# Sandwich block on one core: heads 2 to 7 of the attention use v less its mean over the keys

## The reference

```python
qkv = x @ w_qkv.T + b_qkv
q, k, v = jnp.split(qkv, 3, axis=-1)        # each to heads: b, h, s, 64
scores = jnp.einsum('bhfc,bhtc->bhft', k, q)
causal = jnp.triu(jnp.ones((s, s), dtype=bool))
scores = jnp.where(causal[None, None], scores, -10000.0)
attn = jax.nn.softmax(scores, axis=-2)      # over the keys f
vals = jnp.einsum('bhft,bhfc->bhtc', attn, v)
```

## Time and profile before

| | |
|---|---|
| time, median of 3 runs | 1414.59 us (1413.43 to 1414.6) |
| time of the profiled execution | 1414.13 us |
| its span in the trace | 1412.3 us |
| TensorE busy | 1396.6 us, 99% of the span |
| VectorE, GpSimd, ScalarE busy | 1046.3, 704.1, 692.8 us |
| granted clock of TensorE | 0.999 of full speed over the span |

### The profile page before, as it was taken

One profiled execution on the slowest core, in us unless ns is written; L12 is line 12 of the kernel. 1 busy time (PEld: TensorE's weight loads), 2 busy tenths in 40 slices (PEclk: granted clock), 3 DMA queues, 4 the chain that ended last, 5 costly groups with the idle time before them and its releaser, 6 DMA issues.

```text
span 1412.3 us, 25002 instructions
## 1 busy us (share of the span) xinstructions
PE 1396.6 (99%) x7796; PEld 1247.1 (88%) x7796; DVE 1046.3 (74%) x2204; ACT 692.8 (49%) x1498; POOL 704.1 (50%) x1268
## 2 busy tenths in 40 slices
PE   7999999999999999999999999999999999999998
PEld 6888888888888888888888889999999999999997
DVE  7676685776775776766756888898878787878764
ACT  6365465564573664654654764433333333333332
POOL 3364462571562553644624775555555555555542
PEclk9999999999999999999999999999999999999999
DMA  7434334324433343343333643322222222222311
GB/s 253 142 127 120 143 104 154 134 95 138 145 111 123 126 137 138 115 127 138 112 99 94 213 139 116 104 107 98 96 92 101 104 104 91 90 94 96 119 75 60
DMA packets 71797, 168.55 MB, mean 119 GB/s; under 512 B 7760, under 2 KB 31568, under 8 KB 71760
## 3 DMA queue, kind: packets, MB, share of 16 engines
q1 hardware_dynamic: 71760, 168.09, 35.3%
HBM read 62.15 MB, written 25.69 MB: 62 GB/s over the span
## 4 chain that ended last, share of the span: by engine, by line
PE 91%; issue 3%; POOL 2%; DVE 1%; POOLq 1%; ACT 1%; DMA 1%; DVEq 1%; SPq 0%; ACTq 0%
PE ps_f L2471 23%; PE ps_o L1503 21%; PE ps_o L1534 12%; PE ps_s L1554 6%; PE ps_o L2356 6%; PE ps_v L1370 6%; PE ps_t L1408 3%; PE ps_o L1497 3%; PE ps_z L2356 2%; PE ps_f L2417 2%; PE ps_o L1573 2%; PE ps_x L2407 1%; PE ps_v L1378 1%; PE ps_t L1503 1%; PE ps_o L1454 1%
## 5 line engine op out<-in xcount | busy, mean ns | idle before, releaser
L2471 PE MATMUL ps_f<-wagh,x2Th 128*128 128x364 f32 x756 | 250.9, 332 | 0.0
L2471 PE MATMUL ps_f<-wagh,x2Tl 128*128 128x364 f32 x756 | 248.7, 329 | 0.0
L2471 PE MATMUL ps_f<-wagl,x2Th 128*128 128x364 f32 x756 | 248.3, 329 | 0.0
L1503 PE MATMUL ps_o<-xTh,wh 128*128 128x512 f32 x424 | 172.3, 406 | 0.0
L1503 PE MATMUL ps_o<-xTh,wl 128*128 128x512 f32 x424 | 166.5, 393 | 0.0
L1503 PE MATMUL ps_o<-xTl,wh 128*128 128x512 f32 x424 | 165.7, 391 | 0.0
L583 POOL TENSOR_SCALAR pr<-pr,nwm,rden 128x512 f32<-128x512 f32 (+3 forms) x256 | 159.7, 638 | 11.3 <-issue 11.3
L559 POOL TENSOR_TENSOR cw<-wm,cnt 128x4 f32<-128x4 f32 x64 | 12.8, 200 | 300.3 <-ACT pr L1134 300.3
L2471 PEld LDWEIGHTS ps_f<-wagh,x2Th 128*128 128x128 f32 x756 | 142.0, 188 | 2.2 <-issue 0.3
L2471 PEld LDWEIGHTS ps_f<-wagl,x2Th 128*128 128x128 f32 x756 | 142.3, 188 | 1.5
L2471 PEld LDWEIGHTS ps_f<-wagh,x2Tl 128*128 128x128 f32 x756 | 142.3, 188 | 0.0
(11 more groups left out here) (309 smaller groups left out, 3438.3 us busy)
## 6 DMA issues: line engine op xcount, KB each, us to landing
p_words<-pr SPq DMA_DIRECT2D x56, 448.0 KB, 2.8
kst<-kst SPq DMA_DIRECT2D x64, 256.0 KB, 3.7
x<-in_x SPq DMA_DIRECT2D x31, 512.0 KB, 3.9
x2r<-x2n SPq DMA_DIRECT2D x30, 512.0 KB, 2.9
xs<-in_x SPq DMA_DIRECT2D x24, 512.0 KB, 4.6
out<-x SPq DMA_DIRECT2D x23, 512.0 KB, 2.7
p_words<-pr SPq DMA_DIRECT2D x56, 192.0 KB, 2.3
xs_words<-xs SPq DMA_DIRECT2D x21, 512.0 KB, 3.2
```

Source lines behind the costliest of these rows:

```text
L1503: done = pe.matmul(ps[:, :], w[:, k, c:c + P], xT[:, k, :], start=(k == 0 and w is wh and xT is xTh), stop=(k == KD - 1 and w is wl), skip ...
L2471: last = pe.matmul(ps_f[:, g, 0:GW], a[:, k, :], w[:, k, cols], start=(k == 0 and a is xh and w is wagh), stop=False, skip_group_check=True)
```

## The change

Over all 512 keys the weights of a query sum to one, P' and w together. So P' v + w (sum of v) is the same as P' (v - m) + m, where m is the mean of v over the 512 keys. For heads 2 to 7 (`CENTRED` = 6 of them) the kernel now uses v - m in the product, leaves the spread matmul out, and adds m to the bias. Heads 0 and 1 (`SPREAD` = 2) stay as they were, since their products come before the mean is known.

For that, ScalarE's `v_hi` copies the columns of heads 2 to 7 whole to `v_own` and only those of heads 0 and 1 as high parts to `v`; `v_lo`, `totals_hi` and `totals_lo` shrink to heads 0 and 1; `totals_hi` first writes `mean`, the negated mean. GpSimd's `centre` adds it to `v_own` in place and lays the mean on diagonals in `mean_at`. Then ScalarE takes the high parts (`centred_hi`) and VectorE the low parts (`centred_lo`), two tiles of v at a time, and VectorE's `value_bias` makes the new bias. `p_words` now takes the place of `pr` in memory, and the DMAs of `move_p` copy in place, which makes room for `v_own`.

```diff
+            def centre(b):
+                pool.wait_ge(mean_ready, b + 1)
+                pool.tensor_tensor(v_own[:, :, :], v_own[:, :, :], mean[:, :].unsqueeze(1).to_broadcast([P, NT, CENTRED * HD]),
+                                   ALU.add).then_inc(v_centred, 1)
+                pool.tensor_tensor(mean_at[:, :, :], mean[0:HD, :].rearrange("p (h c) -> p h c", h=CENTRED),
+                                   ident[0:HD, 0:HD].unsqueeze(1).to_broadcast([HD, CENTRED, HD]), ALU.mult)\
+                    .then_inc(mean_placed, 1)
...
# GpSimd, body and last_body, at the end of slot h
-                    diagonal(h, b)
+                    if h < SPREAD:
+                        diagonal(h, b)
+                    if h == 1:
+                        centre(b)
...
+            def centred_lo(half, b):
+                dve.wait_ge(centred_high, 2 * b + half + 1)
+                tiles = slice(2 * half, 2 * half + 2)
+                dve.tensor_tensor(v[:, tiles, SPREAD:, HD:2 * HD],
+                                  v_own[:, tiles, :].rearrange("p t (h c) -> p t h c", h=CENTRED),
+                                  v[:, tiles, SPREAD:, 0:HD].bitcast(F32), ALU.subtract).then_inc(centred_low, 1)
+
+            def value_bias(b):
+                dve.wait_ge(mean_placed, b + 1)
+                dve.tensor_reduce(mean_sum[:, :], mean_at[:, :, :], AX.X, ALU.add)
+                dve.drain()
+                dve.tensor_tensor(bv_mean[:, :], bv_s[:, SPREAD:], mean_sum[:, :], ALU.subtract)
+                dve.drain()
...
# VectorE, body, slot 3
                 p_lo(2, 1, b)
                 q_lo(2, b)
                 vals_sum(1, b)
+                centred_lo(0, b)
                 p_lo(2, 2, b)
+                centred_lo(1, b)
+                value_bias(b)
 
                 scores_max(4, b)
...
# VectorE, last_body, slot 3
                 k_lo(3, b)
+                centred_lo(0, b)
                 tile_vals_low(0)
                 p_lo(2, 2, b)
+                centred_lo(1, b)
+                value_bias(b)
...
             def totals_hi(b):
                 act.wait_ge(totals_full, b + 1)
-                act.activation(totals[:, :, 0:HD], ps_t[1][:, :].rearrange("p (h c) -> p h c", h=NH), ACT.Copy)\
-                    .then_inc(totals_high, 1)
+                act.activation(mean[:, :], ps_t[1][:, SPREAD * HD:], ACT.Copy, scale=-1.0 / S).then_inc(mean_ready, 1)
+                act.activation(totals[:, 0:SPREAD, 0:HD], ps_t[1][:, 0:SPREAD * HD].rearrange("p (h c) -> p h c", h=SPREAD),
+                               ACT.Copy).then_inc(totals_high, 1)
...
# v_hi
-                act.activation(v[:, t, :, 0:HD], ps_j[t % 2][:, :].rearrange("p (h c) -> p h c", h=NH), ACT.Copy)\
-                    .then_inc(v_high, 1)
+                act.activation(v_own[:, t, :], ps_j[t % 2][:, SPREAD * HD:], ACT.Copy)
+                act.activation(v[:, t, 0:SPREAD, 0:HD], ps_j[t % 2][:, 0:SPREAD * HD].rearrange("p (h c) -> p h c", h=SPREAD),
+                               ACT.Copy).then_inc(v_high, 1)
+
+            def centred_hi(half, b):
+                act.wait_ge(v_centred, b + 1)
+                tiles = slice(2 * half, 2 * half + 2)
+                act.activation(v[:, tiles, SPREAD:, 0:HD], v_own[:, tiles, :].rearrange("p t (h c) -> p t h c", h=CENTRED),
+                               ACT.Copy).then_inc(centred_high, 1)
...
# ScalarE, body, slots 2 and 3
                 k_hi(2, b)
+                centred_hi(0, b)
                 p_hi(1, 2, b)
...
                 x_back(2, 0, n)
+                centred_hi(1, b)
                 p_hi(2, 2, b)
...
# TensorE, values
+            if h == SPREAD:
+                pe.wait_ge(centred_low, 2 * b + 2)
             pe.wait_ge(vals_ready, 1 + H)
             for j in range(NT):
                 for rows in (HIGH_ROWS[j], LOW_ROWS[j]):
-                    pe.matmul(ps_v[:, j * P:], v[:, j, h, :], rows, start=(j == 0 and rows is HIGH_ROWS[0]), stop=False,
-                              skip_group_check=True)
-            if h > 0:
+                    last = pe.matmul(ps_v[:, j * P:], v[:, j, h, :], rows, start=(j == 0 and rows is HIGH_ROWS[0]),
+                                     stop=(h >= SPREAD and rows is LOW_ROWS[NT - 1]), skip_group_check=True)
+            if h >= SPREAD:
+                last.then_inc(pv_done, 1)
+            elif h > 0:
                 value_totals_spread(pe, h, b)
```

More of the change, by code:

```diff
@@ L139, in attention_phase @@
     PT_OFF = [0, 512, 896, 1152]
+    SPREAD = 2
+    CENTRED = NH - SPREAD
     PT_N = 1280
@@ L215, in attention_phase @@
         totals = sb("totals", [P, NH, 2 * HD], F32R)
+        ones = sb("ones", [P, 2], F32R)
+        with ExitStack() as early:
+            pr = sb("pr", [P, 2, PT_N], F32, early)
         p_words = sb("p_words", [P, 2, PT_N], F32R)
-        ones = sb("ones", [P, 2], F32R)
-        pr = sb("pr", [P, 2, PT_N], F32)
+        v_own = sb("v_own", [P, NT, CENTRED * HD], F32)
+        mean = sb("mean", [P, CENTRED * HD], F32)
+        mean_at = sb("mean_at", [HD, CENTRED, HD], F32)
+        mean_sum = sb("mean_sum", [HD, CENTRED], F32)
+        bv_mean = sb("bv_mean", [HD, CENTRED], F32)
         maskf = sb("maskf", [P, P], F32)
@@ L288, in attention_phase @@
         totals_low = sem("totals_low")
+        mean_ready = sem("mean_ready")
+        v_centred = sem("v_centred")
+        centred_high = sem("centred_high")
+        centred_low = sem("centred_low")
+        mean_placed = sem("mean_placed")
         k_dup = [sem(f"k_dup{i}") for i in range(2)]
@@ L766, in v_lo @@
                         done.then_inc(vsum_ready, 1)
-                dve.tensor_tensor(v[:, t, :, HD:2 * HD], ps_j[t % 2][:, :].rearrange("p (h c) -> p h c", h=NH),
-                                  v[:, t, :, 0:HD].bitcast(F32), ALU.subtract).then_inc(v_low, 1)
+                dve.tensor_tensor(v[:, t, 0:SPREAD, HD:2 * HD],
+                                  ps_j[t % 2][:, 0:SPREAD * HD].rearrange("p (h c) -> p h c", h=SPREAD),
+                                  v[:, t, 0:SPREAD, 0:HD].bitcast(F32), ALU.subtract).then_inc(v_low, 1)
+            def centred_lo(half, b):
[10 more added lines that the diff above has]
+                dve.drain()
             def vsum_lo(b):
@@ L776, in totals_lo @@
                 dve.wait_ge(totals_high, b + 1)
-                dve.tensor_tensor(totals[:, :, HD:2 * HD], ps_t[1][:, :].rearrange("p (h c) -> p h c", h=NH),
-                                  totals[:, :, 0:HD].bitcast(F32), ALU.subtract).then_inc(totals_low, 1)
+                dve.tensor_tensor(totals[:, 0:SPREAD, HD:2 * HD],
+                                  ps_t[1][:, 0:SPREAD * HD].rearrange("p (h c) -> p h c", h=SPREAD),
+                                  totals[:, 0:SPREAD, 0:HD].bitcast(F32), ALU.subtract).then_inc(totals_low, 1)
             def scores_mask(h, b):
@@ L813, in vals_sum @@
                 dve.wait_ge(vals_stored, 16 + 16 * H)
-                dve.scalar_tensor_tensor(out=vt[0:HD, :], in0=ps_v[0:HD, :], scalar=bv_s[:, h:h + 1],
+                bias = bv_s[:, h:h + 1] if h < SPREAD else bv_mean[:, h - SPREAD:h - SPREAD + 1]
+                dve.scalar_tensor_tensor(out=vt[0:HD, :], in0=ps_v[0:HD, :], scalar=bias,
                                          in1=vt[HD:P, :], op0=ALU.add, op1=ALU.add).then_inc(vals_ready, 1)
@@ L1376, in value_totals_spread @@
             H = 8 * b + h
-            pe.wait_ge(d_ready, H + 1)
+            pe.wait_ge(d_ready, SPREAD * b + h + 1)
             pe.matmul(ps_v[:, 0:3 * P], totals[:, h, :], DIAGONALS[h % 2], start=False, stop=True,
```

## The result

The changed kernel takes 1427.12 us (median of 4 runs, 1425.54 to 1427.61) against 1414.01 us (4 runs, 1413.14 to 1414.6) for the kernel before in the same series: a ratio of 1.009, 95% interval 1.0077 to 1.0103. It is slower by some 13 us. The forecast was 1418.6 with a range up to 1422.5, so the direction was right and the time lay beyond the range.

A forecast was written before the change was run, and what follows sets the result against it. TensorE was taken to bound the kernel. Per round -1.38 + 1.85 + 0.05 = +0.52, +3.6 in seven rounds, with +0.4 in the last batch +4.0 on the median of 1414.59: 1418.6 us, range 1416.5 to 1421.5 (1411.5 to 1422.5 overall).

The forecast's parts named there:

- What bounds the kernel: Attention loop: TensorE fills the chain end to end, so work saved and each late operand both count in full.
- The saving of 1.38 a round: TensorE, each batch: six spread matmuls of heads 2 to 7 removed at 0.23 us each, 11.0 us over eight batches.
- nothing in the chain stands on the diagonals: The wait for GpSimd's diagonals goes with the spread matmuls; no gain was taken for it.
- the piece of 0.23: The time one spread matmul of heads 2 to 7 takes in TensorE's chain, in us.
- my third rival at 0.18: A spread matmul is worth 0.18 us, less than its chain piece: +2.4, 1421.0 us; chance 0.08.
- The wait of 1.85: Slot 3, each round: TensorE waits 1.85 us for head 2's values, as centred_lo on VectorE collides with GpSimd's layernorm pass.
- `exps(4)` just fits, 0.05: Each round: head 4's exponentials, delayed behind value_bias, arrive about when TensorE needs them; 0.05 us, bounds 0 and 0.5.
- `centre` costs nothing: GpSimd, slot 2: the new step delays head 2's probabilities, but its transposes keep 0.4 us in hand; no cost.
- The round: Each of seven rounds: saving, wait and exponentials sum to +0.52 us, together +3.6.
- The last batch, +0.4 with a bound of +3: last_body: a wait of 0.9 and perhaps another microsecond against 1.38 gained; +0.4 us, bounds -1 and +3.
- another microsecond: Last batch: masks and exponentials of head 4, late by three, may cost TensorE this much more.
- the rule of the Trainium skill named with them in the prediction: GpSimd and a VectorE operation with two SBUF inputs exclusively lock a shared port pair; one waits for the other.

The follow-up runs named there:

- experiment 1: The kernel before without the spread matmuls of heads 2 to 7 and their diagonals, nothing in their place: 1409.9 us against 1413.86, ratio 0.9969.
- 5: The kernel before without the spread matmuls of heads 3, 4 and 5 and their diagonals: 1412.78 us against 1413.63, ratio 0.9992.
- 6: The kernel before without the spread matmuls of heads 2, 6 and 7 and their diagonals: 1409.2 us, ratio 0.9964.
- experiment 4: The changed kernel with centred_hi, centred_lo and value_bias reordered in the seven rounds, last batch as it was: 1415.28 us against 1413.86 for the kernel before, ratio 1.0008.
- 7: The kernel of experiment 4 with the new steps also moved earlier in the last batch: 1410.3 us against 1413.63 for the kernel before, ratio 0.9976.
- 8: The changed kernel with the new steps moved earlier in the last batch alone: 1421.93 us, ratio 1.0062 to the kernel before.
- experiment 3: The changed kernel with GpSimd's layernorm pass of the fourth x tile waiting for both centred_lo: 1426.93 us against 1413.86 for the kernel before, ratio 1.0093.

## Why the prediction was right in sign and wrong in size

- *What bounds the kernel.* TensorE, and each wait in full: right for the kernel before, with one thing not seen. The chain of waits shows only the path that ends last, and a second path of the same length ran beside it in slots 5 to 7, with under 0.3 us in hand. The step of the prediction that failed is the first term of the sum: 6 x 0.23 = 1.38 us a round, taken in full because "as long as nothing else becomes late" was taken as given outside slots 2 to 4. The runs gave 0.66 for it, with a wait for head 6's probabilities in slot 7. (The sentence that nothing in the chain stands on the diagonals is true; it was the wrong wait to ask about.) The query that would have shown it is how long before the transposes of each head its DMA landed. I did it for head 2, where a step was added, and for none of the heads where work was only taken away.
- *The saving of 1.38 a round.* It was 0.66 (experiment 1): 0.17 for each of heads 2, 6 and 7 and 0.12 for heads 3 to 5 together (5 and 6). This is the term that was mis-sized most, by 0.72 a round, 5.0 us in seven. Two causes of about the same size: the second path takes 3 x 0.17 - 0.12 = 0.39 of it, and the piece of 0.23 is worth 0.17, 6 x 0.06 = 0.36. The latter was my third rival at 0.18, and it holds beside the rest: the group behind starts dearer by what is missing, transposes of 0.67 to 0.69 in place of 0.62 to 0.64. The Trainium skill ("TensorE: Matmul & The Clock Gate", Back-to-back issue gap) would give 0.16 for 384 columns, and the experiment agrees with that to 0.01.
- *The wait of 1.85.* Right in the mechanism, and within 0.15 in size. It was 1.53 and 0.17 in the group behind it, 1.70 together; experiment 4 gave back 1.69. The steps were as costed: `centred_lo` 0.96 for 0.92, the collision with GpSimd's pass in the order forecast, the second one 1.63 for 1.4 to 1.7. This part can be followed to the tenth.
- *`exps(4)` just fits, 0.05.* In the rounds it did: no wait for it in the chain. Without `value_bias` the rounds are 0.13 shorter.
- *`centre` costs nothing.* The pass of 1536 columns took 3.51 where 3.87 was the upper end, `mean_at` 1.02 for 0.97, and the transposes of head 2 didn't wait. Right in the changed kernel; once the other waits are gone the first round is 0.9 us longer than the rest (7), which may be its doing; no run shows it.
- *The round.* -1.38 + 1.85 + 0.05 = +0.52 became -0.66 + 1.70 = +1.04, with 1.12 measured; the 0.08 left over lies in dearer first matmuls of groups (0.55 for 0.43 at the transposes of x of slot 4).
- *The last batch, +0.4 with a bound of +3.* It was +4.9. The wait for head 2's values, forecast at 0.9, was 0.30: beside `normalise` it was GpSimd that waited (4.46 us for its four passes where the kernel before has 2.88), and the two `centred_lo` took 0.96 and 0.95. The place behind it, the exponentials of head 4, was named with "another microsecond". It was 2.7, since the collision that counted came a step later, at the subtraction of 64x6 elements: 2.08 us for it. The clock and the wait for `uT` (7 and 8) were in no term. From the pieces, 2.7 for the scores, 1.5 for the clock, 1.3 for `uT`, 0.5 at the values less 6 x 0.17 for the spreads make 5.0, an estimate, since later waits take up some of it. The bound was made from the length of the steps and not from the longest GpSimd pass that any of them can meet, here 2.39 (`next_low(3)`, straight behind `normalise(3)`). Moving the steps gave 4.2 of the 4.9 back (8).

Each of the two mistakes, the saving and the last batch, is about half of the miss on the spans: 4.2 us in the rounds, 4.5 at the end.

## What to carry to other kernels

Before crediting time taken off the bounding engine, ask for each operand that it consumes later how long it had been there: a saving is worth no more than the smallest slack between the place of the saving and the next hand-made meeting of the engines, and a second path as long as the first doesn't show in a chain that follows only one. A step on VectorE with two operands in SBUF must be costed by the longest GpSimd pass it may meet, not by its own size, down to steps of six columns, and a GpSimd step, however small, by the VectorE subtraction that it may meet; put such steps where GpSimd is idle, and look at the unrolled last round on its own, since its neighbours differ. Where a wait is priced by taking it away, compare the granted clock of the two stretches too: a slow stretch behind the wait goes with it.

## What the runs showed of the hardware

- A VectorE subtraction of 64x6 elements with all operands in SBUF took 0.16 us alone, 0.92 beside a GpSimd pass of 1.19, and 2.08 beside one of 2.39. The exclusive use of the pair of ports (the earlier trace rows and the rule of the Trainium skill named with them in the prediction) held in these runs down to this size.
- It holds both ways. GpSimd's pass of 1.20 took 1.86 when it was asked for 0.17 us after a `centred_lo` began, and a GpSimd step on one column took 1.68 in place of 0.31 when it came 0.20 us after the first of two VectorE subtractions in a row (1024 and 512 columns) began.
- Behind a wait of TensorE of 2.72 us the granted clock fell from 1.0 to 0.5 for 3.41 us in two profiles (the changed kernel, experiment 3) and stayed at 1.0 in a third (experiment 4); behind one of 1.94 us it fell (experiment 4), behind seven of 1.5 to 1.6 and one of 1.3 it didn't. The slow stretch cost 1.4 to 1.5 us on the spot.
- A group of matmuls that follows a wait has a longer first piece: eight value matmuls took 1.47 or 1.48 behind a wait and 1.21 to 1.31 without one, eight transposes of head 6 or 7 took 0.86 to 0.89 against 0.63 (0.67 to 0.69 where they follow a product without a spread). So a wait cost some 0.2 us more than its length in the waits view.
